# Two stages of a fused transformer block: the last slots of the first interleaved by hand with the first slots of the second

## The chip, the cores and the metric

The kernel runs on one core of one Trainium2 chip. The metric is device time in microseconds (us) for one execution of the whole program. TensorE (PE) multiplies and transposes into PSUM, VectorE (DVE), ScalarE (ACT) and GpSimd (POOL) work on what it leaves, SyncE (SP) issues the loads and stores.

## The reference, cut to what matters

The input `x` has 8 batches of 128 rows by 512 columns. Four residual blocks follow one another; every one normalises `x` first:

```
x = x + tanh(g_xattn[0]) * autocorrelation(layernorm(x), ctx, ctx)
x = x + tanh(g_ffn[0])   * mixture_of_low_rank_experts(layernorm(x), W_base, b_base, W_gate, A, B)
x = x + tanh(g_xattn[1]) * cross_attention(layernorm(x), ctx, mask, Wq, Wk, Wv, Wo)   # 32 heads in 8 groups
x = x + tanh(g_ffn[1])   * ffn_with_lora(layernorm(x), W, A, B)
```

The autocorrelation transforms q and k along the rows, correlates them, takes the 9 largest lags of each column, weights them by a softmax, and applies the lags to v. The expert block chooses 2 of 8 experts for each row. The cross attention projects q for 4 heads and k and v for one group, normalises q and k (RMS), takes scores, softmax, probabilities times v, and the output projection, for each of 8 groups and 8 batches.

## The kernel before, in words

The program has two functions, each with its own `nc.Block()`, so all engines meet between them.

**First stage (`phase_a`), the first two residual blocks.** It runs in slots `b` = 0 to 9; in slot `b` the engines work on batch `b` (lags), `b - 1` (adding the lagged values, routing), `b - 2` (adding the routed output, normalising for the cross attention) and `b + 1` (transforms and correlation). The order on each engine is written out by hand in its `slot(b)`. On TensorE: transpose of `hw` (L483), inverse transform (L486, L487), base products and routed product (L491, L493), q transform (L463), transpose of the lag weights (L501), context transform (L469), lag transforms (L508, L509), transposes of the normalised rows (L514), router (L526), transposes of the next normalised rows `n2` (L533), correlation (L476, L477). DVE picks the lags in `pick_lags` (L566 to L590: maxima, replacements, the copy `ninth<-next` L577, four `scalar_tensor_tensor` `wlag<-rest,elag` L586 with two SBUF inputs, the reciprocal `wrec`), adds to `xres` (L634, L641), and routes (L606 to L624, with the small `rw<-lgr,eg` L619). POOL makes the normalised lag weights `wlagn` (L347), the inverse roots, the sums of the products (L334, L336), the bias (L330), and the low parts `cT_lo` (L319) and `nT_lo` (L325). In slots 8 and 9 there are no more batches to fill all of these places.

Every float32 operand of the second stage is split into a high part in `float32r` and a low part, and a product is three passes (`three_pass`: L854, L855, L856). The first weights are split at the end of slot 7: `first_high` on ACT, `first_low` on POOL (`wkv_lo` L112, `wq_lo` L114), the other three parts of `wq` only after the block boundary (L1083, L1299).

**Second stage (`phase_c`), the last two residual blocks.** `slots(slot)` runs `n` from -2. The unit is one group and one batch, N = 64. TensorE's `slot(n)` is: `scores(n)` (L866, L868), `turn_probs(n - 1)` (L877), `turn_qk(n + 1)` (L904, L905), `project_qkv(n + 2)` (twelve passes of 512 columns for q, twelve of 256 for k and v), `project_out(n - 2)` and `probs_v(n - 1)`. So `slot(-2)` holds one projection alone, `slot(-1)` a `turn_qk` and a projection, `slot(0)` adds scores, and only from `slot(2)` on all six parts are there. Between a projection and its `turn_qk` lies a chain over three engines: squares on ACT (L1032), their sum on DVE (L1138), `+ eps` and the inverse root on POOL (L1257, L1260), the scaling on DVE (L1157).

The printed functions come next, with the line numbers that the profile uses.

## Time and profile before

| | |
|---|---|
| median of 3 runs | 855.87 us (854.86 to 856.57) |
| the profiled execution | 856.37 us, span of its instructions 854.6 us |
| mean granted clock of TensorE | 0.974 |
| TensorE busy | 795.9 us, 93% of the span |
| DVE, ACT, POOL busy | 574.5, 412.2, 364.9 us |

The profile is of one execution. A line is a group of like instructions, named by output and inputs; `pair` is PSUM. A granted clock of 1.00 is the full 2.4 GHz, 0.5 is 1.2 GHz. In square brackets stands the time that the engine was idle just before, and what ended it.

### The profile page before, as it was taken

To read this page: it belongs to the slowest core of one execution; us is meant where nothing else is said; L and a number is where in the kernel's file an instruction comes from. 1 tells how busy PE (TensorE), PEld (TensorE's weight loads), DVE (VectorE), ACT (ScalarE), POOL (GpSimd) and SP (SyncE) were. 2 spreads that over 40 slices of the span, in tenths; PEclk is the share of its full clock that TensorE was granted. 3 is DMA by queue.
4 is the path that set the end of the run, shared out by engine and by line. 5 is a ranking of instruction groups with operands and counts; after the bars stand their busy time and mean duration, and the time that the engine had idled before them with its cause. 6 is when DMAs were issued, how large, how long until landed. Compare 5 with 4: busy or idle time off the path is not lost.

```text
span 854.6 us, 13103 instructions
## 1 busy us (share of the span) xinstructions
PE 795.9 (93%) x4224; PEld 640.7 (75%) x4224; DVE 574.5 (67%) x1283; ACT 412.2 (48%) x1142; POOL 364.9 (43%) x420
## 2 busy tenths in 40 slices
PE   4699997747999999999999999999999999999998
PEld 1355554336788888888888888888888888888776
DVE  3689998214476677666776677666776677767774
ACT  3356455123454455555555446544654455454421
POOL 1356665432542453353236425433542453244432
PEclk9899999778899999999999999999999999999999
DMA  8300100020200030021003000300200021000002
GB/s 293 135 26 26 49 13 2 0 74 1 87 26 13 1 99 25 2 64 48 13 2 99 26 1 17 87 21 2 87 25 15 1 75 50 1 1 13 2 25 75
DMA packets 16979, 34.61 MB, mean 41 GB/s; under 512 B 2320, under 2 KB 2448, under 8 KB 16656
## 3 DMA queue, kind: packets, MB, share of 16 engines
q1 hardware_dynamic: 16912, 33.78, 12.6%
q8 instruction: 35, 0.57, 0.3%
q14 instruction: 32, 0.26, 0.1%
HBM read 31.67 MB, written 2.10 MB: 40 GB/s over the span
## 4 chain that ended last, share of the span: by engine, by line
PE 62%; DVE 6%; POOL 6%; issue 5%; ACT 1%; POOLq 0%; DVEq 0%; ACTq 0%
PE pair L854 17%; PE pair L856 17%; PE pair L855 16%; PE pair L866 4%; PE pair L904 3%; PE pair L877 3%; POOL qkr L1260 2%; POOL probn L1252 1%; PE pair L868 1%; POOL wo_lo L1246 1%; DVE xres L1101 1%; DVE score L1118 1%; PE pair L905 1%; DVE score L1115 1%; DVE oT_lo L1128 1%
## 5 line engine op out<-in xcount | busy, mean ns | idle before, releaser
L1252 POOL TENSOR_TENSOR probn<-prob,erec 128x512 f32<-128x512 f32 x64 | 67.0, 1047 | 164.2 <-DVE erec L1133 164.2
L1138 DVE TENSOR_REDUCE qkss<-qksq 128x5 f32<-128x640 f32 x64 | 52.6, 822 | 106.4 <-ACT qksq L1032 106.4
L1157 DVE TENSOR_TENSOR qkn<-pair,qkr 128x640 f32<-128x640 f32 x64 | 52.8, 824 | 92.7 <-POOL qkr L1260 92.7
L854 PE MATMUL pair<-wq_hi,nT_hi 128*128 128x512 f32 x256 | 110.8, 433 | 3.4 <-PEq L261 3.0
L1025 ACT ACTIVATE prob<-score,nmax 128x128 f32<-128x128 f32 x256 | 99.7, 394 | 16.2 <-DVE nmax L1120 16.1
L1014 ACT ACTIVATE oT_hi<-pair 128x512 fp32r<-128x512 f32 x64 | 38.1, 595 | 140.3 <-PE pair L856 140.3
L854 PE MATMUL pair<-wo_hi,oT_hi 128*128 128x512 f32 x256 | 101.6, 397 | 2.6 <-issue 2.6
L855 PE MATMUL pair<-wq_lo,nT_hi 128*128 128x512 f32 x256 | 103.4, 404 | 0.0
L856 PE MATMUL pair<-wq_hi,nT_lo 128*128 128x512 f32 x256 | 103.3, 404 | 0.0
L856 PE MATMUL pair<-wo_hi,oT_lo 128*128 128x512 f32 x256 | 101.9, 398 | 0.0
L855 PE MATMUL pair<-wo_lo,oT_hi 128*128 128x512 f32 x256 | 101.4, 396 | 0.0
L1032 ACT ACTIVATE qksq<-pair 128x640 f32<-128x640 f32 x64 | 45.2, 707 | 84.6 <-PE pair L856 84.6
L1260 POOL TENSOR_TENSOR qkr<-qkse,neghalf 128x5 f32<-128x5 f32 x64 | 76.7, 1198 | 5.4
L854 PE MATMUL pair<-wkv_hi,cT_hi 128*128 128x256 f32 x256 | 72.6, 284 | 0.3 <-DVE kT L1146 0.3
L855 PE MATMUL pair<-wkv_lo,cT_hi 128*128 128x256 f32 x256 | 72.3, 282 | 0.0
L856 PE MATMUL pair<-wkv_hi,cT_lo 128*128 128x256 f32 x256 | 71.7, 280 | 0.0
L1241 POOL TENSOR_TENSOR wq_lo<-wq_raw,wq_hi 128x512 fp32r<-128x512 f32 x28 | 36.4, 1299 | 77.0 <-ACT wq_hi L1004 77.0
L866 PE MATMUL pair<-kT,qT_hi 128*128 128x256 f32 x256 | 62.4, 321 | 0.0
L854 PEld LDWEIGHTS pair<-wq_hi,nT_hi 128*128 128x128 f32 x256 | 50.1, 196 | 13.6 <-issue 3.2
L856 PEld LDWEIGHTS pair<-wq_hi,nT_lo 128*128 128x128 f32 x256 | 49.8, 195 | 12.8
L1019 ACT ACTIVATE pT_hi<-pair 128x512 fp32r<-128x512 f32 x64 | 38.4, 600 | 43.5 <-PE pair L877 43.5
L854 PEld LDWEIGHTS pair<-wo_hi,oT_hi 128*128 128x128 f32 x256 | 48.1, 188 | 12.8 <-issue 3.4
(180 smaller groups left out, 2015.1 us busy)
## 6 DMA issues: line engine op xcount, KB each, us to landing
wq_raw<-in_wq SPq DMA_DIRECT2D x32, 256.0 KB, 2.8
wo_raw<-in_wo SPq DMA_DIRECT2D x32, 256.0 KB, 2.9
wkv_raw<-in_wkv SPq DMA_DIRECT2D x8, 512.0 KB, 4.7
ctxn<-in_ctx_n SPq DMA_DIRECT2D x8, 256.0 KB, 3.0
ctxt<-in_ctx_t SPq DMA_DIRECT2D x8, 256.0 KB, 2.7
out<-wkv_raw SPq DMA_DIRECT2D x8, 256.0 KB, 2.0
xres<-in_x SPq DMA_DIRECT2D x1, 1280.0 KB, 11.2
wbase<-in_wbase SPq DMA_DIRECT2D x1, 1024.0 KB, 8.4
```

Source lines behind the costliest of these rows:

```text
L854: pe.matmul(out, l_hi, r_hi, start=start, stop=False)
L855: pe.matmul(out, l_hi, r_lo, start=False, stop=False)
L856: return pe.matmul(out, l_lo, r_hi, start=False, stop=stop)
L866: pe.matmul(s_bank[:, h, :, :].rearrange("p i t -> p (i t)"), qT_hi[:, w], kT[:].rearrange("p i t -> p (i t)"), start=True, stop=True, ski ...
L1014: act.activation(oT_hi[:], o_bank[:], ACT.Copy).then_inc(o_h, 1)
L1019: act.activation(pT_hi[:], pt_bank[:], ACT.Copy).then_inc(p_h, 1)
L1025: t = act.activation(prob[:, h, :], score[:, h, :], ACT.Exp, bias=nmax[:, h:h + 1], accum_out=esum[:, h:h + 1])
L1032: act.activation(qksq[:], qk_bank, ACT.Square).then_inc(qk_sq, 1)
L1138: dve.tensor_reduce(qkss[:], qksq[:], AX.X, ALU.add).then_inc(qk_ss, 1)
L1157: dve.tensor_tensor(qkn[:], qk_bank, qkr[:].unsqueeze(2).broadcast_to([P, HG + 1, P]), ALU.mult).then_inc(qk_nat, 1)
L1252: pool.tensor_tensor(probn[:], prob[:], erec[:].unsqueeze(2).broadcast_to([P, HG, P]), ALU.mult).then_inc(normed, 1)
L1260: pool.tensor_tensor(qkr[:], qkse[:], neghalf[:, 0:HG + 1], ALU.pow).then_inc(qk_root, 1)
```

## The change

Both stages come into one `nc.Block()`. The slots 0 to 6 of the first stage stay as they are in order, except for the first weights' splits, which move into them. The slots 7, 8 and 9 of the first stage and the slots -2, -1 and 0 of the second are written out on every engine as one sequence in three parts; `slots(slot)` of the second stage starts at `n` = 1. The projection is cut into `project_q` (by chunks) and `project_kv`. Since both stages now live at once, 60 KB per partition of the first stage's buffers (`kfa`, `kfb`, `op`, `wbase` and others) share their place with buffers that the second stage uses later (`wo_raw`, `wo_hi`, `wo_lo`, the second set of weights, `pT`, `oT`, `score`, `probn`); new waits guard the first use (on `corr`, `o_prod`, `w_norm`, `h_out`, `f_out`). PSUM banks are renumbered in the first stage. ACT's tanh of the gates now stands ahead of the normalisation of batch 0. In the diff's core below, the first list of calls after POOL's `a_slot` is POOL's, then follow ACT's, TensorE's and DVE's.

```diff
--- before.py
+++ after.py
...
-        def first_low(pool):
...
-        def first_high(act):
...
+        with ExitStack() as first:
+            def early(name, shape):
+                return first.enter_context(nc.sbuf_tensor(name, shape, F32))
+            kfa = early("kfa", [P, 2, D])
+            prod1, prod2 = (early(f"prod{i}", [P, D]) for i in range(2))
+            kfb = early("kfb", [P, 4, D])
+            rest8, rest9, elag, wlag = (early(n, [P, CH, P]) for n in ("rest8", "rest9", "elag", "wlag"))
+            op = [early(f"op{i}", [P, D]) for i in range(4)]
+            wbase = early("wbase", [P, CH, D])
+            bcat, bb = early("bcat", [P, D]), early("bb", [P, D])
+            wlagn, wT = early("wlagn", [P, CH, P]), early("wT", [P, D])
+            nx, ctxt = early("nx", [P, D]), early("ctxt", [P, CH, P])
+            ctxn = early("ctxn", [P, 2, D])
+            n1, n1T = early("n1", [P, D]), early("n1T", [P, CH, P])
+        wo_raw = sb("wo_raw", [P, HG, D])
+        wo_hi = sb("wo_hi", [P, HG, D], F32R)
+        wo_lo = sb("wo_lo", [P, HG, D], F32R)
+        wkv_hi1, wkv_lo1 = sb("wkv_hi1", [P, CH * 2 * P], F32R), sb("wkv_lo1", [P, CH * 2 * P], F32R)
+        wq_hi1, wq_lo1 = sb("wq_hi1", [P, CH, D], F32R), sb("wq_lo1", [P, CH, D], F32R)
+        pT_hi, pT_lo = sb("pT_hi", [P, HG * P], F32R), sb("pT_lo", [P, HG * P], F32R)
+        oT_hi, oT_lo = sb("oT_hi", [P, HG * P], F32R), sb("oT_lo", [P, HG * P], F32R)
+        score, probn = sb("score", [P, HG, P]), sb("probn", [P, HG, P])
...
+        wr_bank, wi_bank, k_banks, corr_bank = bank[0], bank[1], (bank[3], bank[2]), bank[4]
+        h_bank, base_bank, route_bank = bank[5], bank[6], bank[7]
+        def n2_bank(b):
+            return wi_bank if b < B - 1 else route_bank
...
+                sp.wait_ge(corr, B)
+                for h in range(HG):
+                    sp.dma_start(wo_raw[:, h, :], wo_d[h]).then_inc(ld_wo[h], 16)
...
+                    if g == 1 and c == 0:
+                        pool.wait_ge(w_fwd, 2 * B)
+                        pool.wait_ge(h_out, B)
+                        pool.wait_ge(h_bias, B)
...
+                    if g == 0 and h == 0:
+                        pool.wait_ge(w_norm, B)
...
+                def a_slot(b):
+                    if has(b - 2):
+                        add_bias(b - 2)
+                    low_turned_ctx(b)
+                    if has(b - 3):
+                        low_rows(b - 3)
+                    if b == 4:
+                        low_wkv(0)
+                    if b in (5, 6):
+                        for c in (2 * b - 10, 2 * b - 9):
+                            low_wq(0, c)
+                    lag_weights(b)
+                    if has(b - 1):
+                        h_scale(b - 1)
+                    if has(b - 2):
+                        g_scale(b - 2)
+                    if has(b + 2):
+                        f_scale(b + 2)
+                    sums(b)
...
+                f_scale(0)
+                f_scale(1)
+                pool.wait_ge(bias_gated, 1)
+                for b in range(B - 1):
+                    a_slot(b)
+                add_bias(5)
+                low_turned_ctx(7)
+                low_rows(4)
+                lag_weights(7)
+                h_scale(6)
+                g_scale(5)
+                sums(7)
+                add_bias(6)
+                inverse_norms(0)
+                h_scale(7)
+                low_rows(5)
+                g_scale(6)
+                add_bias(7)
+                inverse_norms(1)
+                low_rows(6)
+                g_scale(7)
+                norm_probs(0)
+                inverse_norms(2)
+                low_rows(7)
+                low_wkv(1)
...
+                    if g == 1:
+                        act.wait_ge(f_out, B)
...
+                    lag_exponents(b)
+                    if b == 3:
+                        high_wkv(0)
+                    if b in (4, 5):
+                        for c in (2 * b - 8, 2 * b - 7):
+                            high_wq(0, c)
+                    copy_lags(b)
...
+                act.wait_ge(ld_g, 16)
+                act.activation(gate[:], gates_in[:], ACT.Tanh).then_inc(tanhed, 1)
+                normalise(nx[:], 0, f_sc, f_root, f_norm)
...
+                copy_hw(5)
+                high_turned_ctx(7)
+                lag_exponents(7)
+                copy_lags(7)
+                normalise(n1[:], 6, h_sc, h_root, h_norm)
+                copy_rows(6)
+                normalise(n2[:], 5, g_sc, g_root, g_norm)
+                squares(0)
+                route_exponents(6)
+                high_v(0)
+                high_rows(5)
+                copy_hw(6)
+                normalise(n1[:], 7, h_sc, h_root, h_norm)
+                copy_rows(7)
+                act.wait_ge(wqk_done, 2)
+                high_qk(0)
+                normalise(n2[:], 6, g_sc, g_root, g_norm)
+                route_exponents(7)
+                squares(1)
+                high_v(1)
+                high_rows(6)
+                copy_hw(7)
+                high_qk(1)
+                exponents(0)
+                normalise(n2[:], 7, g_sc, g_root, g_norm)
+                squares(2)
+                high_v(2)
+                high_rows(7)
+                high_wkv(1)
...
+                    if n == 0:
+                        pe.wait_ge(f_added, B)
+                        pe.wait_ge(o_prod, 4 * B)
+                        pe.wait_ge(g_copied, B - 1)
...
+                def project_q(n, chunks):
+                    g, even, here = n // B, n // B % 2, at(n)
+                    need(pe, qk_nat, n)
+                    if n == 0:
+                        pe.wait_ge(k_copied, 5 * B)
+                    if n < B:
+                        pe.wait_ge(g_hi, n + 1)
+                        pe.wait_ge(g_lo, n + 1)
+                    for c in chunks:
+                        if n % B == 0:
+                            pe.wait_ge(wq_l, CH * g + c + 1)
+                        t = three_pass(q_bank, nT_hi[:, c, here], nT_lo[:, c, here],
+                                       wq_hi[even * CH + c], wq_lo[even * CH + c], c == 0, c == CH - 1)
+                    return t
+                def project_kv(n):
+                    g, even, here = n // B, n // B % 2, at(n)
+                    need(pe, qk_nat, n)
+                    need(pe, v_h, n)
+                    need(pe, v_l, n)
+                    need(pe, k_l, n)
+                    if n == 0:
+                        pe.wait_ge(k_copied, 5 * B)
+                    if n < B:
+                        pe.wait_ge(ct_hi, n + 1)
+                        pe.wait_ge(ct_lo, n + 1)
+                    if n % B == 0:
+                        pe.wait_ge(wkv_l, g + 1)
+                    for c in range(CH):
+                        w = slice(c * 2 * P, (c + 1) * 2 * P)
+                        t = three_pass(kv_bank, cT_hi[:, c, here], cT_lo[:, c, here],
+                                       wkv_hi[even][:, w], wkv_lo[even][:, w], c == 0, c == CH - 1)
+                    return t
+                def project_qkv(n):
+                    project_q(n, range(CH))
+                    project_kv(n).then_inc(qkv_done, 1)
...
+                turn_hw(5)
+                inverse(6)
+                base_products(5)
+                routed_product(5)
+                project_kv(0)
+                turn_lags(7)
+                project_q(0, (0, 1))
+                lag_transforms(7)
+                turn_rows(6)
+                project_q(0, (2, 3)).then_inc(qkv_done, 1)
+                router(6)
+                turn_out(5)
+                inverse(7)
+                turn_hw(6)
+                base_products(6)
+                routed_product(6)
+                turn_rows(7)
+                turn_qk(0)
+                project_q(1, (0, 1))
+                router(7)
+                project_q(1, (2, 3))
+                project_kv(1).then_inc(qkv_done, 1)
+                turn_out(6)
+                base_products(7)
+                scores(0)
+                turn_hw(7)
+                turn_qk(1)
+                routed_product(7)
+                project_qkv(2)
+                turn_out(7)
+                slots(slot)
...
+                pick_lags(7)
+                add_lagged(6)
+                add_routed(5)
+                dve.wait_ge(ld_norm[0], 16)
+                dve.wait_ge(ld_norm[1], 16)
+                dve.tensor_scalar(wqk[:], norm_w[:, 0:1], float(P) ** 0.5, None, ALU.mult).then_inc(wqk_done, 1)
+                out_products(7)
+                dve.wait_ge(wqk_done, 1)
+                dve.tensor_scalar(wqk[:], wqk[:], norm_w[:, 1:2], None, ALU.mult).then_inc(wqk_done, 1)
+                route(6)
+                sum_squares(0)
+                add_lagged(7)
+                low_v(0)
+                scale_qk(0)
+                add_routed(6)
+                dve.wait_ge(wqk_done, 2)
+                low_k(0)
+                low_q(0)
+                route(7)
+                sum_squares(1)
+                low_v(1)
+                scale_qk(1)
+                dve.wait_ge(ld_mask, 16)
+                mask_and_max(0)
+                low_k(1)
+                low_q(1)
+                add_routed(7)
+                reciprocals(0)
+                sum_squares(2)
+                low_v(2)
+                scale_qk(2)
```

## Rows read from the trace of the kernel before

**Rows 1.** The page's slices, 40 of 21.4 us each: busy tenths and granted clock.
```profile
PE   4699997747999999999999999999999999999998
PEclk9899999778899999999999999999999999999999
```

**Rows 2.** Stretches: window, length, busy us of each engine, granted clock, DMA share, GB/s.
```profile
133.15:205.60 72.45, 49.01 (x176) 31.03 (x176) 27.94 (x89) 21.30 (x47) 30.63 (x36) 0.84 0.07 22
133.15:154.60 21.45, 17.39 (x54) 8.27 (x54) 15.00 (x58) 7.79 (x17) 13.57 (x15) 1.00 0.01 1
154.60:170.10 15.50, 10.96 (x27) 5.92 (x27) 3.12 (x13) 3.87 (x7) 5.20 (x9) 0.67 0.00 0
...
209.88:218.18 8.30, 8.30 (x33) 7.08 (x33) 3.55 (x7) 2.86 (x11) 1.04 (x1) 0.63 0.00 1
221.78:231.68 9.90, 9.90 (x45) 8.25 (x46) 5.19 (x11) 3.78 (x13) 7.74 (x8) 0.83 0.64 185
231.68:845.00 613.32, 609.44 (x3503) 526.39 (x3502) 426.53 (x774) 312.69 (x923) 254.77 (x268) 1.00 0.10 31
```

**Rows 3.** Waits from 133 to 232 us: total us, times, longest.
```profile
PE pair L904 <- DVE qkn L1157: 12.4, 4, 4.3
```

**Rows 4.** Stretches of single steps; engines in order PE, PEld, DVE, ACT, POOL.
```profile
116.84:123.02 6.18, 6.18 (x16) 2.83 (x17) 5.97 (x35) 2.03 (x7) 2.49 (x2) 1.00 0.17 42
117.01:118.73 1.72, 1.72 (x6) 0.76 (x6) 1.69 (x11) 0.89 (x3) 0.65 (x1) 1.00 0.00 0
125.48:127.72 2.24, 2.24 (x9) 1.23 (x9) 1.54 (x4) 1.93 (x4) 1.34 (x5) 1.00 0.00 0
129.44:130.81 1.37, 1.37 (x14) 1.37 (x13) 1.33 (x4) 1.13 (x3) 1.37 (x3) 1.00 0.03 6
231.68:232.54 0.86, 0.86 (x9) 0.86 (x8) 0.86 (x2) 0.60 (x1) 0.00 (x0) 1.00 0.07 19
232.54:232.99 0.45, 0.45 (x6) 0.45 (x6) 0.45 (x2) 0.00 (x0) 0.00 (x0) 1.00 0.00 0
233.46:237.78 4.32, 4.32 (x27) 3.77 (x26) 3.69 (x8) 3.31 (x12) 1.79 (x2) 1.00 0.08 8
```

**Rows 5.** Timeline at the seam: start us, length us, engine, line, instruction.
```profile
157.43 0.67 PE L514 MATMUL pair<-dft,n 128*128 128x128 f32 x4 [2.87 <-ACT n L373]
...
171.63 0.18 DVE L554 BATCH_NORM_AGGREGATE g_mv<-g_stat 128x2 f32<-128x6 f32 x1
...
174.05 0.66 PE L533 MATMUL pair<-dft,n 128*128 128x128 f32 x4 [3.97 <-ACT n L373]
```

**Rows 6.** Timeline of slots 5 and 6: DVE and POOL, and TensorE's transpose.
```profile
98.57 1.27 POOL L330 TENSOR_TENSOR xres<-xres,bb 128x512 f32<-128x512 f32 x1
...
99.28 0.59 DVE L619 SCALAR_TENSOR_TENSOR rw<-lgr,eg 128x8 f32<-128x8 f32 x1 [0.37 <-DVE lgr L616]
...
119.30 1.27 POOL L325 TENSOR_TENSOR nT_lo<-n2T,nT_hi 128x512 fp32r<-128x512 f32 x1
...
119.72 0.88 DVE L577 COPY ninth<-next 128x4 f32<-128x4 f32 x1
...
121.80 0.29 DVE L586 SCALAR_TENSOR_TENSOR wlag<-rest,elag 128x128 f32<-128x128 f32 x1
...
123.03 1.04 POOL L347 TENSOR_TENSOR wlagn<-wlag,wrec 128x512 f32<-128x512 f32 x1 [2.46 <-DVE wrec L590]
...
124.12 0.66 PE L501 MATMUL pair<-dft,wlagn 128*128 128x128 f32 x4
```

**Rows 7.** Timeline: POOL's low part of the first k and v weights.
```profile
149.18 2.35 POOL L112 TENSOR_TENSOR wkv_lo<-wkv_raw,wkv_hi 128x1024 fp32r<-128x1024 f32 x1 [2.10 <-ACT wkv_hi L105]
```

**Rows 8.** Timeline of the start: normalisation, first product, tanh of the gates.
```profile
5.91 0.81 ACT L373 ACTIVATE nx<-xres,f_sc 128x512 f32<-128x512 f32 x1 [3.91 <-POOL f_sc L313]
...
7.66 2.08 PE L463 MATMUL pair<-nx,dft 128*128 128x512 f32 x2 [7.66 <-DMA dft<-in_dft]
7.82 0.21 ACT L448 ACTIVATE gate<-gates_in 128x4 f32<-128x4 f32 x1 [1.10 <-DMA gates_in<-in_gates]
```

More of the change, by code:

```diff
@@ new lines, in flamingo_kernel @@
+        dft = sb("dft", [P, N_DFT, P])
+        wag = sb("wag", [P, CH, ER + E])
+        gates_in = sb("gates_in", [P, 4])
+        f_stat = sb("f_stat", [P, 6])
+        f_mv = sb("f_mv", [P, 2])
+        f_sc = sb("f_sc", [P, 2])
+        n2T = sb("n2T", [P, D])
+        top8 = sb("top8", [P, CH, 8])
+        next8 = sb("next8", [P, CH, 8])
+        ninth = sb("ninth", [P, CH, 8])
+        ntop = sb("ntop", [P, CH])
+        wsum = sb("wsum", [P, CH])
+        wrec = sb("wrec", [P, CH])
+        h_stat = sb("h_stat", [P, 6])
@@ new lines, in flamingo_kernel @@
+        h_mv = sb("h_mv", [P, 2])
+        h_sc = sb("h_sc", [P, 2])
+        lg = sb("lg", [P, 2 * E])
+        lg8 = sb("lg8", [P, 8])
+        two = sb("two", [P, 8])
+        nlg = sb("nlg", [P, 1])
+        eg = sb("eg", [P, E])
+        lgr = sb("lgr", [P, 2 * E])
+        rw = sb("rw", [P, E])
+        rsum = sb("rsum", [P, 1])
+        rrec = sb("rrec", [P, 1])
+        hw = sb("hw", [P, ER])
+        hwT = sb("hwT", [P, P])
+        g_stat = sb("g_stat", [P, 6])
+        g_mv = sb("g_mv", [P, 2])
@@ L791, in phase_c, with xb, has @@
         stored = [sem("d_stored0"), sem("d_stored1")]
+        PICK = 4
+        ROUTE = 8
+        H = P // 2
+        def xb(b):
+            return xres[:, b * D:(b + 1) * D]
+        def has(b):
+            return 0 <= b < B
         def on(n):
@@ L816, in slots @@
         def slots(slot):
-            for n in range(-2, FEED + B + 1):
+            for n in range(1, FEED + B + 1):
                 slot(n)
@@ new lines, in lag_weights, with sums @@
+                def lag_weights(b):
+                    pool.wait_ge(picked, PICK * b + 4)
+                    pool.tensor_tensor(wlagn[:], wlag[:], wrec[:].unsqueeze(2).broadcast_to([P, CH, P]),
+                                       ALU.mult).then_inc(w_norm, 1)
+                def sums(b):
+                    pool.wait_ge(o_prod, 4 * b + 2)
+                    pool.tensor_tensor(op[0][:], op[0][:], op[1][:], ALU.add).then_inc(o_sum, 1)
+                    pool.wait_ge(o_prod, 4 * b + 4)
+                    pool.tensor_tensor(op[2][:], op[2][:], op[3][:], ALU.subtract).then_inc(o_sum, 1)
```

1638 lines of the change are left out of this document (746 added, 892 removed).

## The prediction

> **What bounds the kernel now.** I read first the page's slices: TensorE is busy nine tenths or more nearly everywhere, except in slices 7 to 11, and there the granted clock falls too [rows 1]. So TensorE bounds the kernel, and the dip is the seam of the two stages. The table of stretches puts numbers on it. From 231.68 us to 845.00 us TensorE is busy 609.44 of 613.32 us at full clock: nothing can be won there except by removing products, and the change removes none. From 133.15 us, where the last full slot of the first stage opens, to 205.60 us, where `slot(1)` of the second stage opens with `scores(1)`, TensorE is busy 49.01 of 72.45 us, at a mean clock of 0.84 [rows 2]. Part of those 49 us is work at half speed: 154.60 to 170.10 ran at 0.67. The list of waits names what TensorE waited for at the seam: the normalised q and k (`turn_qk`), 12.4 us in four waits, each behind the chain squares (ACT), sum (DVE), root (POOL), scaling (DVE) [rows 3], and the normalised rows of the last `turn_out`, 3.97 us [rows 5]. These are chains of one batch with nothing of another batch beside them.
>
> **The seam, step by step.** The change issues the same products in one hand-written order. I price them from stretches of full speed [rows 4]: `turn_hw`, `inverse`, `base_products` and `routed_product` together 6.18 us, of which `inverse` is 1.72; lag transforms and `turn_rows` 2.24; `router` and `turn_out` 1.37; four transposes 0.45, so five 0.56; `scores` 0.86; one whole projection of q, k and v 4.32.
>
> First stage from 133.15: two openings of 6.18 and one without `inverse`, 4.46, are 16.82. With `turn_lags(7)` 0.45, lag transforms and `turn_rows(6)` 2.24, two times `router` and `turn_out` 2.74, `turn_rows(7)` 0.45 and `turn_out(7)` 0.45, the stage needs 23.15 us. Second stage: three projections 12.96, two `turn_qk` 1.12, `scores(0)` 0.86, together 14.94 us. The sum is 38.09 us.
>
> Waits that I estimate when I lay the other engines' durations beside this order, one after the other: `inverse(7)` waits some 0.35 us for POOL's two sums. `turn_hw(6)` waits some 0.5 us, since DVE's `route(6)` meets POOL's `add_bias(6)`. `turn_out(7)` waits some 1.2 us: from DVE's aggregate to TensorE's transpose that chain took 174.05 - 171.81 = 2.2 us before [rows 5], and DVE reaches it late, with `mask_and_max(0)`, `low_k(1)` and `low_q(1)` queued ahead of `add_routed(7)`. Behind `turn_out` on TensorE stands `scores(1)`, so the whole queue is 1.2 us late. Together 2.05 us. The other long chains are covered. The chain behind `turn_qk` lasts 4.28 us: the projection of batch 2 ended at 205.60 and `turn_qk(2)` began at 209.88, the bounds of two stretches of [rows 2]. After the projection of batch 0 TensorE has 8.0 us of other work before `turn_qk(0)` (1.37 + 6.18 + 0.45). After that of batch 1 it has 4.9 us: `turn_out(6)` 0.45, `base_products(7)` 3.44 (`inverse` shows 0.43 us for a pass, and it has eight), `turn_hw(7)` 0.16 (6.18 less 14 passes) and `scores(0)` 0.86. If that last cover were gone, `turn_qk(1)` would cost up to 4.28 us.
>
> So `slot(1)` opens 38.09 + 2.05 = 40.1 us after 133.15 instead of 72.45: 32.3 us gained. Inside `slot(1)` the wait for `turn_qk(2)` stays, since `project_out(-1)` doesn't exist to cover it, but `squares(2)` runs beside `turn_out(7)` and starts some 0.65 us earlier against the slot: 0.6 us more, 32.9 us in all. The slow stretches after the waits in `slot(1)` (8.30 us at 0.63) and `slot(2)` (9.90 us at 0.83) [rows 2] I leave as they are, since each follows a wait of over 2 us that stays. If the clock held in `slot(1)`, its 8.30 us would be 4.32 + 0.56 + 0.72 (`probs_v`, a quarter of the 12 passes of q at 0.24 us) = 5.6: a further 2.7 us, kept for the range.
>
> **What the change adds.** (1) The split of the first weights moves from the end of the first stage into slots 4 to 6: `low_wkv(0)` in slot 4, two `low_wq` in each of slots 5 and 6, all on POOL between `low_rows` and `lag_weights`. POOL idles 2.46 us there before `wlagn` [rows 6]; one `low_wkv` takes 2.35 us [rows 7], two `low_wq` of the shape 128x512 take 2 x 1.27. So they just fit, and POOL as such loses nothing. But DVE's instructions meet them. In slot 6 `ninth<-next`, a copy of four columns, took 0.88 us and ended at 120.60, where POOL's `nT_lo` ended at 120.57. In slot 5 `rw<-lgr,eg`, a `scalar_tensor_tensor` of two SBUF inputs, ended at 99.87, where POOL's `xres` ended at 99.84 [rows 6]. DVE's four `wlag` instructions have the same two SBUF inputs, and POOL is idle under all of them now. In the new slot 4, placed on slot 6's times, `low_wkv` would run from 120.54 to 122.89, and the first `wlag`, due at 121.80, waits some 1.0 us. In slots 5 and 6 the first `wlag` meets the end of one `low_wq`, and the second waits for the next: again some 1.0 us. Behind them stand `wrec`, POOL's `wlagn` and `turn_lags`. In slot 6 `wlagn` ended at 124.07 and TensorE began `turn_lags` at 124.12 [rows 6]: there is no slack, so I put 3.0 us on the path. Bounds: 0, if `wlag` isn't held up, and 3 x 1.24 = 3.7, if the first `wlag` waits to 123.04 each time. I take 3.0, as the nearest row (`rw`) was held to the end of POOL's instruction.
>
> The Trainium skill's page "SBUF — State Buffer", section "Who interferes with whom", says that a DVE instruction with two SBUF inputs and a GpSimd instruction that reads SBUF exclude each other for a whole instruction. This rule speaks against the change; by it the sum is the one that I take (827 us), and without it the sum would be 824 us. The row of `rw` agrees for 8 columns; for the 128 columns of `wlag` no row shows it yet.
>
> (2) ACT now computes the tanh of the gates before it normalises batch 0. The gates had landed at 7.82 us, and TensorE began at 7.66 us on an `nx` that was ready at 6.72 [rows 8]. Now `nx` is ready at 7.82 + 0.21 + 0.81 = 8.84 us, so TensorE starts 1.2 us later. All of the first slot hangs on that product, so I take the whole 1.2 us; bounds 0 and 1.2.
>
> (3) Moved at no cost: ACT's `high_wkv` and `high_wq` lie in ACT's wait for the turned lags. The loads of `wo` now wait for the last correlation, but are used only in `slot(1)`, some 40 us later. The new waits (`o_prod`, `w_norm`, `h_out`, `f_out`) ask for events that are past by then. The loop of the long stage has the same body.
>
> **Sum.** The profiled execution took 856.4 us. 856.4 - 32.9 + 3.0 + 1.2 = 827.7 us. It stood 0.5 us above the median, so I forecast 827 us.
>
> **Rivals.** *Waits come back in the seam.* Two more exposures of the 4.28 us chain, at `turn_qk(0)` and `turn_qk(1)`, give 836 us. For it: every hand-over above is a length laid out by hand. Against it: DVE was busy 27.94 us and POOL 30.63 us in the old 72.45 us, so both have room in 40. *DVE isn't held up by POOL*: 824 us, for it only that no row shows `wlag` against POOL. *The change doesn't do what it says*: one wait holds the second stage back until the first is through, 855 to 861 us (the additions of 4.2 us against whatever is left). Against it: none of the events that I followed comes that late. *Slower: TensorE runs the seam at the low clock.* Its 38.1 us of products would take about 76 us, 38 more than forecast, 865 us; it decides against the change once 29 of the 38 us run slowly. For it: 154.60 to 170.10 at 0.67. Against it: that stretch opens with a wait of 2.87 us in one piece [rows 5], while from 133.15 to 154.60 TensorE was idle for 4.1 us in pieces and the clock stayed at 1.00 [rows 2].
>
> **Numbers.** Forecast 0.75, waits back 0.12, DVE not held up 0.08, no effect 0.03, low clock 0.02. Range: down by 3.0 (no hold-up), 1.2 (start) and 2.7 (clock in `slot(1)`) to 820 us; up to the first rival, 836 us. What a measurement of this kernel can't tell from no change is about 0.2%, 1.7 us. Faster holds the first three cases and part of the fourth: 0.96; same 0.01; slower 0.03.
>
> **What would show it.** `scores(1)` starts some 28 us earlier than 205.60, near 177.5. Before it no wait of TensorE is longer than 1.5 us and the clock stays at 1.00. `wlag` instructions of slots 4 to 6 last about 1.2 us instead of 0.29, one in each slot; the first product starts at 8.8 us; the stage from `slot(3)` on takes as long as before. Wrong would be: a wait over 3 us at `turn_qk(1)` or `turn_out(7)`, a low clock before `scores(1)`, or a `wlag` of 0.29 us beside a running POOL.

## The result and the profile after

The kernel after takes 816.08 us (median of four executions, 813.65 to 818.52) where the kernel before takes 855.57: a ratio of 0.9537, 95% interval 0.952 to 0.9554. I had forecast 827 us and a range of 820 to 836. The sign and the mechanism at the seam are as forecast, but the gain is larger than the range allowed.

First the page's slices of the kernel after (20.3 us each), TensorE's busy tenths and granted clock, where [rows 1] had its dip:

```profile
PE   4699999988999999999999999999999999999998
PEclk9899999999999999999999999999999999999999
```

The table of stretches of TensorE in the kernel after (window, length, busy us, granted clock, DMA share, GB/s), cut where the slots of the second stage open, beside [rows 2]:

```profile
135.76:175.25 39.49, 38.13 (x175) 1.00 0.20 67
175.25:184.22 8.97, 7.03 (x48) 1.00 0.00 1
178.76:184.22 5.46, 5.46 (x33) 1.00 0.01 2
184.22:196.02 11.80, 9.70 (x57) 1.00 0.44 136
187.81:196.02 8.21, 8.21 (x44) 1.00 0.63 196
196.02:205.51 9.49, 9.49 (x58) 1.00 0.19 54
196.02:773.50 577.48, 574.85 (x3370) 1.00 0.10 31
```

The same places mark the same work in both traces: the opening of the last full slot of the first stage (133.15 before, 135.76 after), `scores(1)` (205.60 and 175.25), `scores(3)` (231.68 and 196.02) and the end of the span (854.6 and 811.9). So the 42.7 us by which the profiled spans differ come apart as follows:

| part | before | after | gain | forecast |
|---|---|---|---|---|
| start to the last full slot | 133.15 | 135.76 | -2.6 | -4.2 |
| seam, to `scores(1)` | 72.45 | 39.49 | +33.0 | +32.3 |
| slots 1 and 2 of the second stage | 26.08 | 20.77 | +5.3 | +0.6 |
| `slot(3)` to the end | 622.9 | 615.9 | +7.0 | 0 |

The list of TensorE's waits from 135 to 197 us of the kernel after (total us, times, longest):

```profile
PE pair L986 <- DVE qkn L1299: 4.0, 2, 2.1
PE pair L908 <- ACT n L603: 1.2, 1, 1.2
PE pair L852 <- DVE hw L1234: 0.4, 1, 0.4
PE pair L856 <- POOL op L477: 0.2, 1, 0.2
```

Of the 12.4 us of [rows 3], 4.0 are left, both after `scores(1)`. In the seam stand 1.2 us before `turn_out(7)` and 0.2 before `inverse(7)`. Its products take 38.13 us at full clock. That is the 38.09 of the prediction, counted from single steps.

The timeline of the kernel after, at the start, in slot 5 and at the end of the seam (start us, length us, engine, line, instruction, idle time and its releaser), beside [rows 6] and [rows 8]:

```profile
6.72 0.20 ACT L777 ACTIVATE gate<-gates_in 128x4 f32<-128x4 f32 x1 [4.72 <-DMA gates_in<-in_gates]
6.83 0.80 ACT L603 ACTIVATE nx<-xres,f_sc 128x512 f32<-128x512 f32 x1
...
7.78 2.05 PE L832 MATMUL pair<-nx,dft 128*128 128x512 f32 x2 [7.78 <-ACT nx L603]
...
103.34 1.27 POOL L461 TENSOR_TENSOR nT_lo<-n2T,nT_hi 128x512 fp32r<-128x512 f32 x1
...
104.57 2.54 POOL L491 TENSOR_TENSOR wq_lo<-wq_raw,wq_hi 128x512 fp32r<-128x512 f32 x2
...
105.85 1.41 DVE L1186 SCALAR_TENSOR_TENSOR wlag<-rest,elag 128x128 f32<-128x128 f32 x1
...
107.19 0.28 DVE L1186 SCALAR_TENSOR_TENSOR wlag<-rest,elag 128x128 f32<-128x128 f32 x1
...
174.84 0.66 PE L908 MATMUL pair<-dft,n 128*128 128x128 f32 x4 [1.15 <-ACT n L603]
```

The first `wlag` of the slot takes 1.41 us instead of 0.29: it ends at 107.26, just behind POOL's second `wq_lo` (107.11). At the start, `nx` now follows `gate`, and the first product follows `nx`.

Four questions were left: which gain belongs to the interleaving, what the hold-up and the start cost, where the 7.0 us of the long stage come from, and how much of the gain in slots 1 and 2 stays in other executions.

### The profile page after: what moved, and what is told of

Read it like the earlier page. It is cut to its first block, busy times and chain, and to the rows that moved or that the text cites. A ratio compares the mean times of both kernels' runs of the same rounds, so it can differ in the third digit from the quotient of the medians.

```text
span 811.9 us, 13195 instructions
## 1 busy us (share of the span) xinstructions
PE 774.1 (95%) x4224; PEld 631.9 (78%) x4224; DVE 577.2 (71%) x1283; ACT 412.1 (51%) x1142; POOL 364.9 (45%) x420
## 4 chain that ended last, share of the span: by engine, by line
PE 68%; DVE 17%; POOL 7%; issue 6%; ACT 1%; DMA 1%; SPq 0%; POOLq 0%; DVEq 0%; ACTq 0%
PE pair L825 17%; PE pair L826 17%; PE pair L827 17%; PE pair L924 4%; PE pair L937 3%; PE pair L986 3%; POOL qkr L512 2%; POOL probn L504 2%; PE pair L926 1%; DVE prod L1160 1%; DVE wlag L1186 1%; POOL wo_lo L498 1%; DVE xres L1243 1%; DVE score L1260 1%; DVE rest L1170 1%
## 5 line engine op out<-in xcount | busy, mean ns | idle before, releaser
L825 PE MATMUL pair<-wq_hi,nT_hi 128*128 128x512 f32 x256 | 105.8, 413 | 0.0
L827 PE MATMUL pair<-wq_hi,nT_lo 128*128 128x512 f32 x256 | 100.4, 392 | 0.0
L826 PE MATMUL pair<-wq_lo,nT_hi 128*128 128x512 f32 x256 | 100.2, 391 | 0.0
L827 PE MATMUL pair<-wo_hi,oT_lo 128*128 128x512 f32 x256 | 99.6, 389 | 0.0
L491 POOL TENSOR_TENSOR wq_lo<-wq_raw,wq_hi 128x512 fp32r<-128x512 f32 x32 | 41.7, 1306 | 75.3 <-ACT wq_hi L668 75.3
L825 PE MATMUL pair<-wkv_hi,cT_hi 128*128 128x256 f32 x256 | 72.7, 284 | 0.5 <-DVE kT L1288 0.5
L926 PE MATMUL pair<-kT,qT_lo 128*128 128x128 f32 x256 | 56.9, 222 | 0.0
L827 PEld LDWEIGHTS pair<-wo_hi,oT_lo 128*128 128x128 f32 x256 | 48.1, 188 | 10.6
```

Source lines behind the costliest of these rows:

```text
L491: pool.tensor_tensor(wq_lo[k], wq_raw[:, c, :], wq_hi[k].bitcast(F32), ALU.subtract).then_inc(wq_l, 1)
L825: pe.matmul(out, l_hi, r_hi, start=start, stop=False)
L826: pe.matmul(out, l_hi, r_lo, start=False, stop=False)
L827: return pe.matmul(out, l_lo, r_hi, start=False, stop=stop)
L926: t = pe.matmul(s_bank[:, h, 0, :], qT_lo[:, w], kT[:, 0, :], start=False, stop=True, skip_group_check=True)
```

## Experiments

Runs compared with the kernel before had it beside them on the same chip (medians 854.43, 855.73, 855.24, 857.1 and 855.64 us). "Period" is the time from one slot's `scores` to the next in the long stage; in the 53 slots from `scores(3)` to `scores(56)` it is the same to 0.03 us, so one profile tells it. Two kernels, `after_low` and `rows_off128`, are exceptions and are named below.

**The interleaving alone.** `in_turn` keeps the single block, the handed-over buffers and the early weights, and issues the last batches of the first stage and the first of the second one after the other, on all engines. The core of its diff is TensorE's order:

```
+                turn_hw(7)
+                routed_product(7)
+                turn_out(7)
+                project_qkv(0)
+                turn_qk(0)
+                project_qkv(1)
...
-                project_q(0, (0, 1))
...
-                project_q(0, (2, 3)).then_inc(qkv_done, 1)
```

> This is the changed kernel with its hand-written part put in turn again: on every engine first what is left of slots 7, 8 and 9 of the first stage, then slots -2, -1 and 0 of the second, in the order of the kernel before. One block, buffers, banks and the early split of the weights stay. Theory that the interleaving itself earns the time: the seam from turn_hw(5) to scores(1) goes from 39.5 to about 70 us, the clock falls in slots 1 and 2 again (some 4 us), and the time is about 849 us. Rival theory, that the single block and the handing over give a good part of it: 835 us or less.

Measured: 843.92 us (ratio 0.987, 0.9855 to 0.9886), 5 us better than expected. `scores(1)` stands at 201.51 us, some 26 us later than in the kernel after, and the medians are 28 us apart. TensorE's waits from 135 to 230 us of `in_turn` show what came back. The stretches below them are its seam, from `turn_hw(5)` to `scores(1)`, and its slots from `scores(0)` on:

```profile
PE pair L982 <- DVE qkn L1289: 12.3, 4, 4.2
PE pair L904 <- ACT n L601: 5.6, 2, 4.0
```

```profile
137.18:201.51 64.33, 45.43 (x176) 0.89 0.12 41
190.85:201.51 10.66, 7.41 (x40) 0.84 0.01 2
201.51:212.84 11.33, 8.54 (x46) 0.85 0.00 1
212.84:226.29 13.45, 11.35 (x58) 0.87 0.45 138
226.29:235.77 9.48, 9.48 (x57) 1.00 0.08 29
```

The seam takes 64.33 us here, 72.45 before and 39.49 after. So the order of the calls is worth 24.8 us of the 33.0 at the seam, and the single block with its early splits the other 8.1. The low clock in slots 1 and 2 is back with the waits: 24.8 us for the two, where the kernel after has 20.8. But the long stage keeps the new pace (9.48, before 9.61). So that pace has nothing to do with the interleaving.

**What sets the pace of the long stage.** A slot of it has the same instructions in both kernels. The stretches of TensorE in the kernel before, for the 53 slots, for one slot, for its 12 passes of 512 columns of `project_out` and its 12 of the q product:

```profile
231.68:741.40 509.72, 509.72 (x2970) 1.00 0.11 34
231.68:241.29 9.61, 9.61 (x57) 1.00 0.11 30
...
237.78:240.59 2.81, 2.81 (x14) 1.00 0.22 81
233.46:236.34 2.88, 2.88 (x15) 1.00 0.00 0
```

and in the kernel after, the same 53 slots and the same passes:

```profile
196.02:698.77 502.75, 502.75 (x2969) 1.00 0.12 34
202.08:204.82 2.74, 2.74 (x14) 1.00 0.22 81
197.81:200.64 2.83, 2.83 (x15) 1.00 0.00 0
```

The 53 slots gain 6.97 us, 0.13 us each (9.617 us in the mean before, 9.486 after), and TensorE never waits in them. A pass of `project_out` follows the last in 0.228 us instead of 0.234, at the same granted clock and with no wait. What differs is where the operands lie, since the single block allocates in another order. I first suspected the alignment to 128 bytes: the weights of before lie at 96 modulo 128, those of after at 0. `before_aligned` adds to the kernel before two unused stretches:

```
+        pad = sb(top, "pad", [P, 8])
...
+        pad2 = sb(st, "pad2", [P, 8])
```

and `after_shift64` shifts every later buffer of the kernel after by 64 bytes.

> This is the kernel before with two pads of 32 bytes per partition, and nothing else: wq_hi, wq_lo, wkv, wo_hi and wo_lo move from 96 to 0 bytes past a multiple of 128, pT and oT from 64 to 0. Placement theory: TensorE's passes of 512 columns over these operands fall from 0.234 to 0.228 us apart, so a slot of the long stage takes 9.49 instead of 9.61 us, and the 64 slots give about 7 us: 848.5 us. Rival theory, that the faster pace comes with the single block or with the order of the instructions: 855.6 us and 9.61 us for a slot.

> This is the changed kernel with one pad of 64 bytes per partition ahead of all its buffers, and nothing else: every operand that lay on a multiple of 128 bytes now lies 64 past one. Placement theory, with 128 bytes as the step: a slot of the long stage goes from 9.49 back to about 9.61 us, and the time from 816 to about 823 us. If 64 bytes are the step, or the placement has nothing to do with it: 816 us and 9.49 us.

Measured: 852.04 us (0.9975, 0.9959 to 0.9991) with a period of 9.59, and 816.98 us (0.955, 0.9527 to 0.9573) with 9.49. Both refute that theory: aligning the operands in the kernel before brought 0.02 us of the 0.12, and the shift of everything costs nothing. The next pair puts the buffers of before at the places of after, by reserving them in the same order, and changes the place of the rows in the kernel after (`after_low`):

```
+        placed = {}
+        def place(stack, name, shape, dt=F32):
+            placed[name] = stack.enter_context(nc.sbuf_tensor(name, shape, dt))
...
+        def sb(stack, name, shape, dt=F32):
+            if name in placed:
+                return placed[name]
```

> The kernel before (two blocks, in turn) with its SBUF buffers at the addresses of the kernel after: weights, turned probabilities and turned outputs below, the turned rows and contexts above them. No instruction is changed. If the place of the operands sets the pace of the 512-column passes, the slot period of the long stage falls from 9.61 to 9.49 us and the time from 854.4 to about 847.5. If it is something in the single block or its instruction stream, the period stays at 9.61 and the time within 853 to 856.

> The kernel after with the turned rows and contexts allocated first, as before has them (they lie below the weights then; the weights start 64 bytes off). If the place of the operands sets the pace, the slot period rises from 9.49 towards 9.61 us and the time from 816 to about 823. If it is the single block, the period stays at 9.49 and the time at 814 to 818.

Measured: `before_placed` 848.46 us (0.9913, 0.9891 to 0.9935) and `after_low` 817.88 us (0.9554, 0.9533 to 0.9575), period 9.53 in six slots of eight and 9.46 and 9.49 in the other two. That is a part of the rise to 9.61 that was expected. The stretch of one slot in `before_placed`:

```profile
231.05:240.54 9.49, 9.49 (x58) 1.00 0.12 28
```

No instruction of it differs from before, and it has the whole of the new pace (its 53 slots take 502.75 us, as in the kernel after). So places set the pace. The remaining runs ask which property of them. All but `before_256` were executed once: that is enough for the period, but their times have no interval. `rows_off64` and `rows_off128` put 64 or 128 unused bytes ahead of the turned rows and contexts, `rows_between` allocates these between the query weights of odd and of even groups, `after_low0` is `after_low` with 64 bytes more. The edit of `rows_off64`, and that of `rows_between` (five lines moved up; `after_low` moves them further up, ahead of all weights, with the small buffers behind them):

```
+        pad64 = sb("pad64", [P, 16])
         xres = sb("xres", [P, B * D])
```

```
+        xres = sb("xres", [P, B * D])
+        nT_hi = sb("nT_hi", [P, CH, B * P], F32R)
...
         wkv_hi = [sb("wkv_hi0", [P, CH * 2 * P], F32R), wkv_hi1]
...
-        xres = sb("xres", [P, B * D])
-        nT_hi = sb("nT_hi", [P, CH, B * P], F32R)
```

> The kernel after with 64 unused bytes between the weights and the turned rows: the rows and contexts lie 64 bytes off the weights' alignment, all else stays. If the alignment of one operand against the other sets the pace of the 512-column passes, the slot period rises from 9.49 towards 9.6 us (one look, the period is read from the profile). If not, it stays at 9.49.

> The kernel after with the turned rows and contexts allocated between the odd groups' query weights (below them) and the even groups' (above them); everything stays 0 modulo 128. If what counts is on which side of the rows, or how far from them, the weights lie, the slots of even groups take longer than those of odd groups (9.55 to 9.6 against 9.49 us). If only the alignment counts, all take 9.49.

> The kernel with the rows allocated first, as after_low, which had 9.53 us, but with 64 bytes more, so that all operands are 0 modulo 128 as in the kernel after. If the misalignment made the 0.04 us, the period is 9.49; if the place did, it is 9.53 again.

`rows_between`: 9.49 in odd and even groups, 815.1 us. On which side of the rows the weights lie doesn't count. `after_low0`: 9.54 with weights, rows, `pT`, `v` and `oT` at 0 modulo 128, 818.01 us; the alignment to 128 is out. But modulo 256 its weights lie at 0 and its rows at 128, while in the kernel after both lie at 128. `rows_off64`: 9.46, 812.72 us; both theories had missed that one. The third set tests the addresses modulo 256. `before_256` is the kernel before with three unused stretches, its order of buffers untouched:

```
+        pad = sb(top, "pad", [P, 40])
...
+        pad2 = sb(st, "pad2", [P, 24])
...
+        pad3 = sb(st, "pad3", [P, 16])
```

`after_low256` is `after_low0` with 128 bytes more, and `rows_off128` the reverse test on the kernel after.

> The kernel before with three unused stretches (160, 96 and 64 bytes) between its buffers and nothing else changed: each operand of the 512-column passes then has the address modulo 256 that it has in the kernel after (128, v 64), in the order of buffers of before. If the addresses modulo 256 set the pace, the slot period falls from 9.61 to 9.49 us and the time to about 848, as in the run that took over all places. If the order or the distance of the buffers counts, it stays at 9.59 or 9.61 and 852 to 856.

> The kernel with the rows allocated first (9.54 us with the weights at 0 modulo 256 and the rows at 128), with 128 bytes more, so that all are 128 modulo 256 as in the kernel after, and v 64. By the addresses modulo 256 the period is 9.49; by the order of the buffers it is 9.54 again.

> The kernel after with 128 bytes between the weights and the rows: rows at 0 modulo 256, weights at 128, the rest as in after. By the addresses modulo 256 the passes of the query product slow from 0.229 to about 0.233 us each, 12 of them in a slot: a period of 9.54 us. If only the alignment modulo 128 counts, it stays at 9.49.

`before_256` takes 848.37 us (0.9889, 0.9864 to 0.9915), `after_low256` 816.65 and `rows_off128` 819.8. Their slots, in that order, are rows of each kernel's table of stretches; for `rows_off128` they are two neighbours:

```profile
231.67:241.16 9.49, 9.49 (x58) 1.00 0.17 53
```

```profile
208.63:218.12 9.49, 9.49 (x57) 1.00 0.10 29
```

```profile
209.23:218.77 9.54, 9.54 (x57) 1.00 0.10 27
218.77:228.28 9.51, 9.51 (x57) 1.00 0.11 30
```

The first two came out as the addresses modulo 256 say. `rows_off128` did on average only: its slots alternate between 9.54 and 9.51 us, 9.53 in the mean of the 53.

All twelve programs together (addresses within a partition modulo 256; moving operands are the weights and `pT`, stationary ones the rows, `v` and `oT`). No trace shows addresses. They are counted from the order and the sizes of the allocations, each start rounded up to 32 bytes, with 128 taken for the first address in all of them:

| kernel | wq, wo | rows | pT | v | oT | period |
|---|---|---|---|---|---|---|
| before | 224 | 128 | 64 | 64 | 64 | 9.61 |
| before_aligned | 0 | 128 | 128 | 96 | 128 | 9.59 |
| before_placed, before_256, after, rows_between, after_low256 | 128 | 128 | 128 | 64 | 128 | 9.49 |
| after_shift64 | 192 | 192 | 192 | 128 | 192 | 9.49 |
| after_low | 192 | 128 | 192 | 64 | 192 | 9.53 (six of eight slots) |
| after_low0 | 0 | 128 | 0 | 128 | 0 | 9.54 |
| rows_off128 | 128 | 0 | 128 | 64 | 128 | 9.54 and 9.51 in turn |
| rows_off64 | 128 | 192 | 128 | 128 | 128 | 9.46 |

Five programs with the same addresses modulo 256 and otherwise different places have one period. The shift of all by 64 keeps it, which speaks for the places against each other. Equal ones are good, but not the best.

The addresses modulo 256 are not the whole rule. From one batch to the next all operands move by multiples of 512 bytes, so neighbouring slots of `rows_off128` have the same addresses modulo 256, and yet they differ by 0.03 us. And in `after_low` weights and `oT` both lie at 192, as far from each other as in `after_shift64` (both 192) and in the kernel after (both 128), but its 12 passes of `project_out` take 2.79 us where those two have 2.75 and 2.74:

```profile
214.28:217.07 2.79, 2.79 (x14) 1.00 0.30 86
```

Something beside a pass's own two operands modulo 256 must bear on it. Higher address bits, or the places that the other engines use at the same time, are two candidates; no run separates them. The 12 passes of q and the 12 passes of 256 columns of k and v in a slot of `rows_off64`:

```profile
207.74:210.63 2.89, 2.89 (x15) 1.00 0.00 0
210.63:212.00 1.37, 1.37 (x14) 1.00 0.16 19
```

The q product lost 0.06 us there (2.83 in the kernel after) and that of k and v gained 0.07 (1.44 in the kernel after, from 200.64 to 202.08). Why a pass is slower at some places was not found.

**Hold-up and start.** `one_per_slot` spreads POOL's six pieces of 128x512 over slots 1 to 6. `both_undone` keeps slots 4 to 6, moves the second piece of each behind the slot's sums, and takes ACT's tanh back behind the first `nx`. The core of the first, then of the second:

```
-                    if b == 4:
-                        low_wkv(0)
...
+                    if b in (1, 2):
+                        low_half(b - 1)
+                    if b >= 3:
+                        low_wq(0, b - 3)
```

```
                     if b in (5, 6):
-                        for c in (2 * b - 10, 2 * b - 9):
-                            low_wq(0, c)
+                        low_wq(0, 2 * b - 10)
                     lag_weights(b)
...
                     sums(b)
+                    if b in (5, 6):
+                        low_wq(0, 2 * b - 9)
...
+                normalise(nx[:], 0, f_sc, f_root, f_norm)
                 act.wait_ge(ld_g, 16)
                 act.activation(gate[:], gates_in[:], ACT.Tanh).then_inc(tanhed, 1)
-                normalise(nx[:], 0, f_sc, f_root, f_norm)
```

> This is the changed kernel with the split of the first weights spread over slots 1 to 6: at most one POOL instruction of 128x512 stands between low_rows and lag_weights in each slot (two halves of wkv in slots 1 and 2, the four parts of wq in slots 3 to 6). Theory that DVE's wlag instructions are held up by POOL's: each of slots 4 to 6 gets back its 1.1 us, wlag lasts 0.3 instead of 1.4 us, and the time falls by 3.2 us against the changed kernel, 816.1 to about 813 us. Rival theory, that the 3.2 us are POOL's own lateness with wlagn or something else of these slots: no change, or a part of it lost again in slots 1 to 3.

> The kernel after with its two losses undone: of each pair of pieces of the low weight halves that GpSimd makes in slots 4, 5 and 6, one stays before the lag weights and one goes behind the slot's sums; and ScalarE normalises the first batch before it waits for the gates. If the hold-up is what makes these slots 17.3 to 17.4 us long, no first wlag is over 0.3 us and the three slots take 16.3 each: 3.2 us less. If the gates' wait delays the start, the first product no longer follows the gates' landing and stands at 7.7 us: 0.1 to 1.2 less. Together 812 where the kernel after has 816. Rival: the pieces behind the sums delay the next slot's context half instead (its copy starts late by up to 1.3 us) and the time stays at 816.

> The version with both losses undone, a second time, for its interval: 814 to 815 us by the first, 0.951 of before. In its profile the hold-ups stay away; the slot behind the last piece (slot 7) may be 0.7 us longer than 16.3 again.

`one_per_slot`: 816.29 us (0.9552, 0.9538 to 0.9566), no gain. `both_undone`: 814.83 us (0.9511, 0.9486 to 0.9536) where 812 was expected, and, the second time, 814.43 (0.9526, 0.9501 to 0.955). The kernel after, on the chip of the first, took 817.51 us (`after_again` below), so the gain is some 2.7 us, and the intervals overlap; the traces decide better than the times. The stretch from the first `wlag` of slot 3 to that of slot 7 (the slots count from 0), all engines (PE, PEld, DVE, ACT, POOL), in the kernels before, after, `both_again` and `one_per_slot`:

```profile
72.71:138.12 65.41, 63.32 (x254) 35.38 (x253) 62.10 (x231) 37.00 (x79) 40.64 (x57) 1.00 0.08 23
```

```profile
72.10:140.72 68.62, 63.31 (x254) 35.36 (x253) 65.33 (x230) 39.07 (x83) 47.93 (x62) 1.00 0.13 39
```

```profile
72.13:138.30 66.17, 63.30 (x254) 35.36 (x253) 62.85 (x230) 39.05 (x83) 47.98 (x63) 1.00 0.15 46
```

```profile
75.70:140.96 65.26, 63.32 (x254) 35.39 (x253) 61.96 (x231) 36.98 (x79) 44.30 (x61) 1.00 0.14 45
```

TensorE's work is the same in all four. The hold-up costs 68.62 - 65.41 = 3.2 us, seen in DVE's busy time too (3.2 more). Both new orders remove it there: POOL does the same work and no first `wlag` of slots 3 to 7 is over 0.29 us. `one_per_slot` paid for it earlier, as the timelines of its slots 1 and 2 show:

```profile
40.38 1.38 DVE L1193 SCALAR_TENSOR_TENSOR wlag<-rest,elag 128x128 f32<-128x128 f32 x1
...
56.87 1.28 POOL L482 TENSOR_TENSOR wkv_lo<-wkv_raw,wkv_hi 128x512 fp32r<-128x512 f32 x1
57.28 0.90 DVE L1184 COPY ninth<-next 128x4 f32<-128x4 f32 x1
```

In slot 1 the piece (from 40.32 us on) met the first `wlag` again. In slot 2 POOL has no `nT_lo` yet, so the piece meets the copy of four columns instead (0.90 us; 0.17 in the same slot of the kernel after). From the first `wlag` of slot 1 to that of slot 2 it takes 19.00 us instead of 17.19; slot 3's is then reached in 16.32 instead of 16.80. So the moved pieces cost 1.3 us there. The first product came 1.2 us later (8.96), and the slot behind it took 17.87 us where the kernel after had 16.79 (16.6 to 18.0 over all profiles). In all the first `wlag` of slot 3 stands at 75.70, 3.6 us later, which spends the 3.4 us that the stretch gives back. Slot 1 of the second stage was slow in this execution as well (10.56 us). `both_again` loses 0.76 us of the 3.2 again, in the last of these slots. Its timeline there:

```profile
130.15 1.30 POOL L499 TENSOR_TENSOR wq_lo<-wq_raw,wq_hi 128x512 fp32r<-128x512 f32 x1
131.40 1.27 POOL L466 TENSOR_TENSOR xres<-xres,bb 128x512 f32<-128x512 f32 x1
131.78 0.92 DVE L1240 SCALAR_TENSOR_TENSOR rw<-lgr,eg 128x8 f32<-128x8 f32 x1
...
133.34 0.33 PE L863 MATMUL pair<-dft,hw 128*128 128x128 f32 x1 [1.16 <-DVE hw L1245]
```

The moved piece pushes POOL's `add_bias` back onto DVE's `rw`, which again ends with POOL's instruction (132.70 and 132.67), and TensorE waits 1.16 us for `hw`.

The start in `both_again`, timeline:

```profile
5.74 0.81 ACT L614 ACTIVATE nx<-xres,f_sc 128x512 f32<-128x512 f32 x1 [3.74 <-POOL f_sc L440]
6.45 0.19 ACT L789 ACTIVATE gate<-gates_in 128x4 f32<-128x4 f32 x1
...
6.69 2.05 PE L843 MATMUL pair<-nx,dft 128*128 128x512 f32 x2 [6.69 <-ACT nx L614]
```

**How much stays in other executions.** `after_again` is the kernel after unchanged.

> The kernel after unchanged, beside the others. The gates' landing is expected to differ from execution to execution (6.7 to 7.9 us in the profiles so far) and the first product with it. If the full clock in slots 1 and 2 of the second stage belongs to the dense seam, its profile shows slots of 8.97 and 11.80 us again; if it is chance, the slot of 11.80 is 13.4 long in this or other executions, and the time of the executions lies at 814 or at 818.

Measured: 817.51 us (0.9551, 0.9529 to 0.9572). Its stretches of slots 1 and 2:

```profile
177.15:186.14 8.99, 7.06 (x47) 1.00 0.00 1
186.14:199.54 13.40, 11.30 (x57) 0.87 0.46 138
```

The gates landed at 7.41 us here and the first product began at 8.46. Over the thirteen profiles with the interleaved order (`best` below among them), slot 1 took 8.96 to 9.04 us in eleven and 10.56 in two; slot 2 took 11.8 us in six and 13.2 to 13.4 us in seven. Of the first four executions of the kernel after, those at a mean clock of 0.994 took 813.65 and 814.22 us, those at 0.987 and 0.991 took 818.52 and 817.93. The trace of `after_again` is 3.5 us longer than that of the kernel after: 1.6 us in slot 2 and 1.9 before slot 3 of the first stage, of which the later gates are 0.7. So about half of the profiled executions give back the 1.6 us of slot 2. In `before_256`, which is not interleaved, slot 2 took 11.81 us too, so the interleaving is not needed for that. Slot 1 is another matter: the five profiles of kernels that are not interleaved (`before`, `before_aligned`, `before_placed`, `before_256`, `in_turn`) have 11.3 to 12.6 us, and none of the thirteen is over 10.56.

**The best version.** `best` is `both_undone` with the 64 bytes of `rows_off64`.

> The version with both losses undone, and the rows and contexts 64 bytes further up as in rows_off64, whose one look had a period of 9.46 us with the weights at 128, the rows at 192 and the turned values at 128 modulo 256. If the addresses modulo 256 set the pace whatever the rest of the program, the period is 9.46 again and the time 1.7 us below the 814.6 of the version with both losses undone: 813. If equal addresses modulo 256 were what makes the passes fast, 9.46 was chance and it is 9.49.

Measured: 813.0 us (811.02 to 813.38; 0.9497, 0.9475 to 0.9518), as expected. Its slot:

```profile
204.13:213.60 9.47, 9.47 (x57) 1.00 0.10 28
```

Its slots take 9.46 and 9.47 us in turn. It is 0.4% below the kernel after by the ratios, and the intervals just part; from `both_undone` (0.9511, 0.9486 to 0.9536) the times don't separate it.

## Why the prediction was wrong, point by point

*Seam.* Right: 33.0 us gained where 32.3 stood in the sum. The products took 38.13 us (38.09 counted), and `turn_out(7)` waited 1.15 us (1.2). Of the other small waits less came: in all 1.4 us of TensorE's idle time where 2.05 stood. The low clock of 154.60 to 170.10 [rows 2] is gone with the waits. `in_turn` shows what does it: the order of the calls 24.8 us of the 33.0, the single block with the early splits 8.1. The prediction did not separate these two.

*Hold-up.* Right: 3.2 us (3.0 in the sum). The first `wlag` waits until POOL's instruction ends, 1.26, 1.41 and 1.42 us long in slots 4, 5 and 6. The rule of the Trainium skill's "SBUF — State Buffer", section "Who interferes with whom", held for 128 columns as it had for 8.

*Start.* The step was right; what failed in it is that it took the landing of the gates as fixed at 7.82 us. Over the eighteen profiles on record they landed between 6.45 and 8.91 us. With the tanh ahead (eleven profiles) the first product begins 1.05 us behind the start of the tanh. With the normalisation ahead (seven) it waits in six for the landing of `dft` [rows 8], some 0.16 us before that start. So within one execution the order costs an estimated 1.2 us, as forecast. The profile of the table shows 0.1 (7.78 against 7.66) because its gates landed 1.1 us earlier than before. What the first slots make of it differs too: the first `wlag` of slot 3 came at 72.10 us where it came at 72.71 before. It came at 72.1 to 74.7 us, 73.5 in the mean, in ten profiles with the tanh ahead (without `one_per_slot`), and at 72.1 to 73.4, 72.7 in the mean, in the seven others. So the order costs 0.8 us on average, and the table's execution was the luckiest of the ten.

*Slots 1 and 2.* The step that left the slow stretches "as they are, since each follows a wait of over 2 us that stays" failed for slot 1. The wait of 1.94 us for `qkn` stayed, the clock did not fall, and `slot(1)` lasted 8.97 us. It had 2.7 us for that in the range only. Before, that wait was the last of a row of idle stretches; after, TensorE comes out of 38.13 busy us in 39.49. I had tied the clock to the last wait alone. That the dense seam keeps the clock up is argued, not shown: `in_turn` takes the seam's order away and has 11.33 us, but two of the thirteen interleaved profiles have a slow stretch in this slot as well. For slot 2 the step is open: it holds in seven of the thirteen profiles. The profile that I decompose is one of the fast half, 2.4 us below the median.

*Long stage.* This is the step that made the range fail: "The loop of the long stage has the same body", priced at 0, and "nothing can be won there except by removing products". It gave 7.0 us, 0.13 us in each of 53 slots. The body is the same, but its operands moved when the two blocks' allocations became one, and their places set the pace of the passes. `before_256` gains it with 320 unused bytes and nothing else. Which property of the places counts is known in part only: equal addresses modulo 256 gave equal periods in five programs, but they don't explain all the others. None of the rivals had a mechanism for the long stage, and no bound of the range stood for it.

With 7.0 us for the places and 2.7 to 4.7 for the clock of slots 1 and 2, the sum would have been 816 to 818 us.

## What to carry to other kernels

A change that merges blocks or moves an allocation also moves operands, and a stage that "isn't touched" can change its pace by 1%. Compare one slot of each untouched stage before pricing it at nothing, and ask how many times it repeats: 0.13 us times 53 was a sixth of this gain. An idle chain at a seam cost twice here, once in the wait and once in the clock of the work behind it, so a dense order gave back more than its waits. When POOL's idle time is filled, lay the new instructions beside DVE's with two SBUF inputs and its short copies. A piece that ended before them cost nothing; one that ran under them held the first of them up until its end, 1.0 to 1.1 us each time. And a time that hangs on the landing of a load at the start belongs to one execution: compare it over several profiles.

## What the runs showed that I had not expected

- Passes of 512 columns at granted clock 1.00, without a wait, follow each other in 0.234 or 0.228 us (stretches of 12: 2.81 and 2.74 us) by the places of the buffers. The slot's period lay between 9.46 and 9.61 us over eight sets of addresses modulo 256.
- In `rows_off128` neighbouring slots with the same addresses modulo 256 took 9.54 and 9.51 us in turn.
- Kernels with weights, rows, `pT` and `oT` all at 0 modulo 128 had 9.49, 9.54 or 9.59 us.
- A wait of TensorE of about 2 us was followed by a low clock in some executions of a program and by full clock in others: slot 2 of the second stage took 11.8 or 13.4 us with the same instructions.
- The load of the gates, four columns, had landed by 6.45 us in one execution and landed at 8.91 in another (`before_256`), and what waits for it moves by as much.
